# A graph kernel on one core: border edge tiles gathered once for two products, edge terms later in pass one, attention one-hots made by ScalarE

## The reference

```python
x = x + gcn3(layernorm(x))        # three graph convolutions, each followed by batch norm
x = x + moe_ffn(layernorm(x))     # 8 experts, the best 2 for each node
x = x + gat(layernorm(x), edge_attr, src, dst)   # attention over edges, 8 heads
x = x + topk_ffn(layernorm(x))    # half of the tokens of each block
# gcn, one layer, with a self loop on every node:
h = h @ W
out = segment_sum(h[src] * (dinv[src] * dinv[dst])[:, None], dst) + b
# gat:
e = leaky_relu(eh[src] + (edge_attr @ W_e . attn_e) + et[dst])
a = exp(e - e_max[dst]) / denom[dst]
rst = segment_sum(ft[src] * a, dst) + bias
```

## Time and profile before

| | |
|---|---|
| time, median of 3 runs | 6595.78 us (6589.96 to 6596.86) |
| profiled execution, its own time | 6588.06 us |
| its span, first to last instruction | 6586.3 us |
| mean granted clock of TensorE | 0.777 of full speed |
| busy: PE, PE weight loads | 4555.0 us (69%), 3428.4 us (52%) |
| busy: DVE, ACT, POOL | 2857.5 us (43%), 2013.4 us (31%), 3462.2 us (53%) |
| DMA | 790.56 MB, mean 120 GB/s |
| gcn: first gather of the passes | at 113.7, 1361.8 and 2585.2 us |
| attend: its gathers | 4892 to 6139 us |

### The profile page before, as it was taken

How to read it: one execution, slowest core, us unless ns; L and a number is a source line. 1 busy time by engine, 2 the same in 40 slices (tenths; PEclk the granted TensorE clock), 3 DMA queues, 4 the chain that set the end, 5 groups by cost and what they waited for, 6 DMA issues and landing times. The chain is left out here.

```text
span 6586.3 us, 82423 instructions
## 1 busy us (share of the span) xinstructions
PE 4555.0 (69%) x21018; PEld 3428.4 (52%) x21019; DVE 2857.5 (43%) x7377; ACT 2013.4 (31%) x5278; POOL 3462.2 (53%) x3588
## 2 busy tenths in 40 slices
PE   2666666656666666566666665999966776777799
PEld 1555555534444443333344454999954555555566
DVE  4333333333333333333333352333346777777745
ACT  2333333333333333233333332444431111111122
POOL 3666666656666665666666624222225666666101
PEclk7777777767776776677777757999977777777899
DMA  6444444445555554444444434222244444444201
GB/s 195 114 119 118 118 119 119 119 136 161 167 170 165 165 165 138 118 144 130 120 120 121 121 120 131 37 35 36 36 139 128 141 142 141 142 141 138 90 1 39
DMA packets 484768, 790.56 MB, mean 120 GB/s; under 512 B 208029, under 2 KB 337814, under 8 KB 477622
## 3 DMA queue, kind: packets, MB, share of 16 engines
q0 software_dynamic: 179904, 468.85, 27.8%
q1 hardware_dynamic: 304502, 317.59, 14.8%
HBM read 591.79 MB, written 194.31 MB: 119 GB/s over the span
## 5 line engine op out<-in xcount | busy, mean ns | idle before, releaser
L981 POOL DMA_INDIRECT rows<-node_rows,psrc x2496 | 2369.0, 949 | 1328.5 <-issue 605.5
L1247 PE MATMUL ps<-rows,hot 128*128 128x257 f32 x4992 | 1820.2, 508 | 1280.1 <-DVE shared L1062 773.7
L1247 PEld LDWEIGHTS ps<-rows,hot 128*128 128x128 f32 x4992 | 1148.5, 254 | 1791.0 <-issue 1595.6
L1062 DVE TENSOR_TENSOR shared<-shared,ps 128x257 f32 x2496 | 1056.5, 423 | 2311.6 <-remote 1238.8
L2184 POOL DMA_INDIRECT rows<-attn_table,psrc x832 | 791.5, 951 | 536.3 <-issue 218.5
L1179 ACT ACTIVATE hot<-iota_f,pdl 128x128 f32<-128x128 f32 x2496 | 758.8, 388 | 141.9 <-remote 94.1
L2477 PE MATMUL ps<-rows,hot 128*128 128x264 f32 x1664 | 636.7, 538 | 209.5 <-DVE rows L2285 142.7
L2477 PEld LDWEIGHTS ps<-rows,hot 128*128 128x128 f32 x1664 | 403.7, 259 | 356.0 <-DVE rows L2285 154.6
L1817 POOL DMA_INDIRECT resid<-feat,slot_node x105 | 165.1, 1572 | 622.2 <-DVE feat L1832 619.3
L2306 DVE TENSOR_TENSOR sums<-sums,ps 128x264 f32 x832 | 356.8, 429 | 222.3 <-remote 87.8
L1934 PEld LDWEIGHTS ps<-feat 128*128 128x128 f32 x3360 | 393.3, 193 | 8.4 <-DVE feat L1861 2.4
(11 more groups left out here) (458 smaller groups left out, 4518.0 us busy)
## 6 DMA issues: line engine op xcount, KB each, us to landing
slot_rows<-blank SPq DMA_DIRECT2D x112, 520.0 KB
hot_table<-hot SPq DMA_DIRECT2D x104, 512.0 KB
hot<-hot_table SPq DMA_DIRECT2D x52, 1024.0 KB
rows<-node_rows,psrc POOLq DMA_INDIRECT x2496
feat<-in_edge_attr_dram SPq DMA_DIRECT2D x832, 32.0 KB
feat<-slot_rows SPq DMA_DIRECT2D x105, 130.0 KB
rows<-attn_table,psrc POOLq DMA_INDIRECT x832
node_rows<-shared SPq DMA_DIRECT2D x99, 128.5 KB
```

The lines of the kernel that those rows point to most:

```text
L981: g.indirect_dma_start(rows[:, n % RING, :], None, tables[k % 2], bass.IndirectOffsetOnAxis(ap=psrc[:, n:n + 1], axis=0)).then_inc(row_sem ...
L1062: v.tensor_tensor(row, row, ps[banks(k, i)[h * G + b]][:, 0:F + 1], ALU.add).then_inc(added.h, 1)
L1247: pe.matmul(ps[cycle[s]][:, 0:F + 1], hot[:, 2 * half + h, b, :], rows[:, slot, :], start=True, stop=True).then_inc(aggregated.h, 1)
```

## The change

- **Border tiles once.** The gathers of a pass are one for each of the ET = 782 edge tiles instead of one for each of 832 pairs. The products are reordered: products 0 to 95 (BOTH) are those of the 48 edge tiles on borders (SHARED_TILES), two for each tile, from the same buffer; the other 736 follow in the sorted order of node tiles. The buffer of an odd product comes from a table (`product_slots_of`, eight register loads for each half of the first six iterations). RING grows from 32 to 48. Gather 48 waits until product 95 is done, gather n from 96 on until product n is done, which is the product of gather n − 48; in passes two and three the first gather waits for all products of the pass before too.
- **LAG 4 to 7.** Four node tiles are closed after the last iteration of a pass instead of one.
- **Edge terms.** None in the first six iterations of pass one; the 52 steps lie in the 46 others, six of which do two, the second one after the iteration's products.
- **One-hots of the attention.** `hot_table` is gone, its stores in pass two and its loads in attend() with it. ACT makes the one-hots in attend(), 16 `Abs` and two `Relu` for each group of 16 pairs, two groups ahead: the first half between `keep_marks` and `weigh`, the second after `expand_changes`.
- **Tables.** The pair tables for attend() are made first, in natural order, saved to DRAM (`pair_cols`, 1.4 MB) and loaded back in the experts phase; product tables take their place for gcn(). Making these adds some sixty small DVE operations in edge_tables() (drains in place of semaphores), seven indirect gathers on POOL in degrees(), and 14 transposes, seven matmuls and six ACT copies in first_table(). The `bn_stats` move: 12 in degrees() ahead of `hit`, 37 behind it.
- The clearing of rows in pass two starts with a `blank` set in that pass; several small buffers share memory.

```diff
-RING = 32
+RING = 48
+SHARED_TILES = NT - 1
+BOTH = 2 * SHARED_TILES
...
-    SEEN_EARLY = 30
+    SEEN_EARLY = 0
+    SEEN_MID = 12
...
+                    for b in range(ETB):
+                        g.indirect_dma_start(prod_edges[:, b, :], None, edge_table,
+                                             bass.IndirectOffsetOnAxis(ap=prod_tile_i[:, b:b + 1], axis=0)).then_inc(prods_in.h, 16)
...
+                    see_rows(v, SEEN_EARLY, SEEN_MID)
...
-                    see_rows(v, SEEN_EARLY, NT)
+                    see_rows(v, SEEN_MID, NT)
...
-        LAG = 4
+        LAG = 7
+        BANK_LAG = 4
...
+            def edge_steps(i):
+                wait = BOTH // (2 * G)
+                upto = lambda n: max(n - wait, 0) * ITERS // (ITERS - wait)
+                return range(upto(i), upto(i + 1))
...
+                            g.wait_ge(aggregated.h, k * NPAIR)
-                        for n in range(NPAIR):
-                            if k > 0 or n >= RING:
-                                g.wait_ge(aggregated.h, k * NPAIR + n - RING + 1)
+                        for n in range(ET):
+                            if n == RING:
+                                g.wait_ge(aggregated.h, k * NPAIR + BOTH)
+                            elif n >= BOTH:
+                                g.wait_ge(aggregated.h, k * NPAIR + n + 1)
+                            at = 2 * n if n < SHARED_TILES else n + SHARED_TILES
                             g.indirect_dma_start(rows[:, n % RING, :], None, tables[k % 2],
...
-                    def keep_hot(i, half):
-                        for h in range(2):
-                            sp.wait_ge(onehot_ready.h, HALVES + 2 * i + h + 1)
...
-                        take(k, NT - 1)
+                        for j in range(ITERS - LAG, NT):
+                            if j > ITERS - LAG:
+                                v.wait_ge(y_turned.h, k * NT + j)
+                            take(k, j)
+                            if j > ITERS - LAG:
+                                stats(k, j - 1)
...
+                            if p >= BOTH or p % 2 == 0:
+                                n = min(p - SHARED_TILES, ET - 1) if p >= BOTH else p // 2
+                                pe.wait_ge(row_sem[n % RING].h, landed(k, n))
+                                row = rows[:, n % RING, :]
+                            else:
+                                row = rows_of(rows, places[b])
...
+                        for e in terms[1:]:
+                            for h in range(2):
+                                edges.turn(pe, 2 * e + h, e, h)
+                                edges.multiply(pe, 2 * e + h, h)
...
+                    sp.dma_start(cols[:], pair_cols).then_inc(cols_in.h, 16)
...
-                        sp.dma_start(hot[:, u].rearrange("p j n -> p (j n)"), hot_table[n]).then_inc(hot_in[u].h, 16)
...
+                    def mark(n, u, half):
+                        if n >= 4:
+                            a.wait_ge(summed.h, 8 * (n - 3))
+                        for b in range(G * half, G * half + G):
+                            op = a.activation(hot[:, u, b, :], iota_f[:], ACT.Abs, bias=pdl[:, n * AG + b:n * AG + b + 1], scale=-1.0)
+                        op.then_inc(hot_step.h, 1)
+                        a.wait_ge(hot_step.h, 2 * n + half + 1)
+                        part = hot[:, u, G * half:G * half + G]
+                        a.activation(part, part, ACT.Relu, bias=ones[:, 0:1], scale=-1.0).then_inc(hot_set.h, 1)
...
+                        if there(n + 2):
+                            mark(n + 2, (u + 2) % 4, 0)
                         weigh(n, u)
                         if there(n + 1):
                             expand_changes(n + 1)
+                        if there(n + 2):
+                            mark(n + 2, (u + 2) % 4, 1)
```

More of the change, by code:

```diff
@@ L433, in _ @@
[L433 to L438, removed]
+                    v.tensor_tensor(counts[:, 0, :], ps[0][:, 0:NT], counts[:, 1, :], ALU.subtract)
@@ new lines, in _ @@
+                    v.drain()
+                    v.tensor_tensor(steps[:, 0, :], key[:, 1:NT], key[:, 0:NT - 1], ALU.subtract)
+                    v.drain()
+                    dp = drow[:, :, 0]
+                    v.tensor_tensor(taken[:], passed[:, :, 0:NT - 1], steps[:, 0:1, :].to_broadcast([P, ETB, NT - 1]), ALU.mult)
+                    v.tensor_reduce(dp, passed[:, :, 0:NT - 1], AX.X, ALU.add)
+                    v.drain()
+                    v.tensor_reduce(tile_of[:], taken[:], AX.X, ALU.add)
@@ new lines, in _ @@
+                    v.drain()
+                    v.tensor_tensor(steps[:], sorted_rows[:, 1:3, 1:NT], sorted_rows[:, 1:3, 0:NT - 1], ALU.subtract)
+                    node = prod_row[:, :, PROD]
+                    v.memset(prod_row[:], 0.0)
+                    for k, res in ((0, prod_tile[:]), (1, node)):
+                        v.drain()
+                        v.tensor_tensor(taken[:], passed[:, :, 0:NT - 1], steps[:, k:k + 1, :].to_broadcast([P, ETB, NT - 1]), ALU.mult)
+                        v.drain()
+                        v.tensor_reduce(res, taken[:], AX.X, ALU.add)
+                        v.drain()
+                        v.tensor_scalar(res, res, sorted_rows[:, 1 + k, 0:1], None, ALU.add)
@@ L953, in gcn @@
             hidden_kept = sem("hidden_kept")
-            hot_kept = [sem(f"hot_kept{u}") for u in range(4)]
             roots = [Rsqrt(var[:], rstd[:], tmp[:]) for _ in range(3)]
             def banks(k, i):
-                return FOUR if k == 0 or (isinstance(i, int) and i < LAG) else SIX
+                return FOUR if k == 0 or (isinstance(i, int) and i < BANK_LAG) else SIX
             def used_before(cycle, at):
@@ L1328, in _ @@
                         iterations(pe, k, first, iteration)
-                        turn_done(k, NT - 1)
-                        hidden(k, NT - 1)
+                        for j in range(ITERS - LAG, NT):
+                            turn_done(k, j)
+                            hidden(k, j)
     gcn()
@@ L2409, in chain @@
                             expand_changes(n + 1)
+                        if there(n + 2):
+                            mark(n + 2, (u + 2) % 4, 1)
                     def begin():
+                        for half in range(2):
+                            mark(0, 0, half)
                         expand_changes(0)
@@ L2414, in begin @@
                             keep_marks(0, 0, half)
+                        for half in range(2):
+                            mark(1, 1, half)
                         chain(0, 0)
```

365 lines of the change are left out of this document (242 added, 123 removed).

## The result

The changed kernel takes 6678.62 us (median of four, 6676.69 to 6681.19) beside 6593.16 for the kernel before: a ratio of 1.0132, 95% interval 1.0117 to 1.0146. It is slower by 85 us. I had forecast 6605 us, a change that a measurement hardly tells from none. The profiled execution is 6676.69 us against 6588.06, so 88.6 us are to be found, where my sum has +10.

The account below looks back on a forecast made before the run. It took the chain of PE's products and DVE's adds, slowed by the gathers, as the bound. 8 + (−10 + 10 + 11) + 2 × (−16 + 11) + 1 + 0 = +10 gave 6598 on the profiled time, 6605 on the median; range 6430 to 6680.

Parts of the forecast that it names:

- The stop: Passes of gcn(): gather 48 waits for product 95, border work about 115 us, a second slow opening, tail 35 us.
- −16: Passes two and three: each 1201 us from first gather to last add against 1218 today.
- the doubled edge steps: Pass one: six extra steps of 6 us, 36 us if all exposed, mostly in PE's idle time: +10 (0 to 40).
- The −10 of the same pass: Pass one: gain from border sharing, less than −16 because its second opening has edge terms.
- Nothing: Attend: ACT's one-hots, 7.2 us a group, lie in idle gaps and cost nothing; ends −10 and +16.
- rival 1: Passes: the gather sets the pace, 150 saved give −216, −164 with costs: 6432 us; chance 0.15.
- Rival 1's own sign: Opening of the passes: a border phase of 60 to 70 us would show that the gather sets the pace.
- my 33: Ends of the three passes: four node tiles closed late under LAG 7, 11 us a pass (6 to 14).
- the deeper ring absorbs no stall: Steady stretch: pace unchanged by the ring of 48; the rival that it absorbs stalls had −50, 6555 us, chance 0.13.
- The slot registers: Border halves, 12 times a pass: PE's slot-number loads lie behind the adds, priced at nothing; 7 us a pass if uncovered.
- rival (4): Openings of the passes: second opening streams 64 gathers or more, 20 us a pass longer plus 5: +75, 6680; chance 0.08.
- the 106 us border: Border phase: paired products might lift the clock in the first 60 us, giving 106 us, 9 a pass less.

Follow-up runs that it names:

- the first set: One-chip runs of edits to the changed kernel (single edge steps, no stop) and the kernel before (attention's one-hots alone, fill of 16); the kernel before took 6597 us.
- the slower set: The runs of the second set, where the kernel before took 6646 us, 0.8% slower than 6593.
- the second set: One-chip runs of LAG 7 alone in the kernel before, and of the changed kernel without sharing or with joined edits (fills 16, 8); the kernel before took 6646 us.
- the third set: Changed kernel with stop and fill 16, joined kernel (fill 8), changed kernel itself: 5765.76, 5752.65, 5764.38 us, beside 5828.92 for the kernel before.

## Why the prediction was wrong

The result is 78 us over the forecast of the profiled execution (88.3 for 10): 23.7 in pass one, 31 in passes two and three, 16.7 in attend, some 7 elsewhere. Three terms of the sum were too small, and beneath them one picture was wrong.

**The stop: "border work lasts about 60 + 54 = 115 us" and "The tail is longer ... 35 then".** That border products would wait for their 96th product and the slow opening come twice I had, with its place. Gather 48 came 127 and 125 us after the first in passes two and three, not 115: 16 adds were made in the first 60 us, not 20, and the others took 0.84 us each, not 0.72. The tail was 40 and 39 us, not 35. The 734 gathers between took 1050 and 1053 us for the 1051 of the sum. 12 + 5 and 10 + 4 us: so −16 became −1 and 0. The run without the stop shows what it costs, 49, 48 and 52 us in the three passes, more than the changed kernel's whole 85 us.

**Pass one: the doubled edge steps.** I priced six steps of 6 us as mostly hidden, +10 in all. Single steps give back 29 us, and each doubled one shows 8 to 10 us behind it. PE's idle time in the steady stretch does not hide them. The −10 of the same pass was about right: with single steps it is 6 us shorter than before.

**Attend: "Nothing".** I let ACT's one-hots lie in gaps of 7.60 and 3.31 us at nothing, with +16 as the upper end. Attend took 16.7 us more. The edit alone shows 11 us in the first set, while in two other sets kernels with and without it take the same. So this term was too small by 16.7 in the result, and how much of that is the one-hots stays open.

**The pace.** The picture that failed is in "What bounds the kernel now": "What bounds a pass is this chain, slowed by the gathers". I read a full ring as a bound consumer. In POOL's timeline, of which the earlier trace rows has two rows, gathers go at 1.2535 us, and two to four waits, 3 us in all for 16 gathers, make the rest of the pace of 1.4373. Then a gather left out is worth 1.25 to 1.44 us. I had this as rival 1 with a chance of 0.15 and argued against it with the full ring. Runs: without the stop, fifty gathers fewer are worth 64 to 68 us in two comparisons; without sharing, passes are 24 us longer than the changed kernel's in spite of its stop (15 with the slower set's 0.8% taken off); with half the ring, the gathers take the same time. The pace does not follow the depth: POOL was allowed 16, 32 or 48 gathers ahead in the first set, and 16 gathers took 23.0 to 23.1 us in the steady stretch; with 8, 16, 32 or 48 in the second set they took 23.2 to 23.3. Why late signals make just this pace at every depth is not shown. In my sum this error did little, since 734 gathers at 1.4373 come out the same by either picture; it hid what the stop would take away. Rival 1's own sign, a border phase of 60 to 70 us, did not come while the stop was there.

**What held.** Start +10 for +8, the gaps between passes +9.9 and +11.5 for +11, and the LAG edit alone shows +37.5 in all for my 33; that the one-hots' 54 MB bring nothing in pass two; that the deeper ring absorbs no stall (23.0 us for 16 before and after). The slot registers cost nothing that shows. While POOL is silent 32 border products with their loads pass in 20.3 us, with DVE 0.2 us later at the start of each eight:

```profile
2722.90:2743.20 20.30, 13.54 (x32) 1.00 0.01 2
```

My rival (4) named 6680 us, beside the measured 6678.62, and that is luck: the second opening's 32 adds took 106 us instead of 93, but by the 1050 and 1053 us above nothing of it reached the pass. The granted clock stayed at 0.56 in the first 60 us of the border phase, near the lower level of 1.2 GHz, and rose to 0.87 in the stop, where PE's products follow each other without gathers. That sustained work lifts it, as the Trainium skill says ("TensorE: Matmul & The Clock Gate", Part 1), the trace bears out, but products in pairs were not such work while their signals came late; the 106 us border that this would have given did not come.

**The condition.** The sign was the other one in the third set. The trace of before could have told that the passes hang on something apart from the instructions: 1238.8 us of DVE's idle time end "remote", and I took it for a law of streaming gathers. Without it the same program runs some 765 us shorter (5829 for 6593). What sets the condition stays open: it was one and the same within each set of runs, with and without a profile, and the two conditions met on one chip. Where the held-back signals wait was not tried; the bytes that the gathers move are excluded, by one run.

## What to carry to other kernels

A full ring does not say that the consumer is the bound: compare the pace with a change in depth (one number) before pricing a producer's work at nothing. Compare kernels within one set of runs: attend with the same one-hots took 1249.5 us in one set and 1266.8 in the next. When one transfer feeds two products, let the wait follow the buffer that is reused; a wait for the whole phase costs the time in which the producer could have run, and the slow start once more. A producer held 8 or 16 steps ahead gave up no pace here and cut the tail of passes two and three from 23 or 39 us to 7 to 14; but in a quick condition a fill that is too short costs what it saves.

## What the runs showed that I had not expected

The same kernel, with the same durations of each instruction (POOL's gather 949 and 947 ns, DVE's add 423 and 423), took 6586 us in one set and 5830 in another, on one chip 5831 and 6642. The difference lies where POOL issues indirect transfers: of 757 us, 541 are in the three passes, 188 in attend and 29 between them; behind attend's gathers 446.4 us became 445.4. And it goes with idle time that ends "remote", which DVE's adds have in the one condition and not in the other. In the trace of before these are 262 waits of 4.7 us on average (at most 11.3), and in nine of ten the product to be added had ended at least 4.1 us before its add began. In the quicker condition the waits end with PE's product, and nine of ten of these adds begin within 3.1 us of its end. I read this as signals of PE that reach DVE late while gathers are issued; no run changed the signals alone. A change can be slower by 1.3% in the one condition and faster by 1.1% in the other; the kernel without the stop is faster in both, 0.989 and 0.976.
